# A mixture-of-experts stage whose gathered rows are split into fp16 halves before they are turned instead of after

## The chip, the cores and the metric

The kernel runs on one core of one Trainium2 chip. The metric is the device time of one execution in microseconds. The kernel before takes 682.88 us (median of 3 runs, 682.84 to 685.06).

## The reference

The input is `x`, 16 batches of 224 rows of 512 fp32 numbers. Two blocks follow each other, each with a residual and a gate `tanh(g)`:

```
x = x + tanh(g_xattn) * attention_like(layernorm(x))     # two products with a context of 750 rows per batch, gelu between them
f = layernorm(x)                                         # 3584 rows of 512
scores = softmax(f @ gate_w); top 2 of 8 experts
y = sum over the 2 experts e of a row:  ( silu((s*f) @ w1[e]) * ((s*f) @ w3[e]) ) @ w2[e]      # 512 -> 256 -> 512
x = x + tanh(g_ffn) * y
```

`s` is the score of the row for that expert. The change lies in the second block.

## The kernel before

The kernel has two phases. In the first, a loop over 16 batches does the attention-like block, norms the rows a second time, chooses the experts and writes the normed rows `xf` and a route table to DRAM. In the second phase, 63 blocks of 128 rows, each of one expert, go through the expert's three matrices. Blocks 0 to 26 are written out one by one (`PEEL2 = 27`), and what is left of the last batches (routing, second norm, the map of the later blocks) is put between them (`between(b)`); blocks 27 to 62 run in a loop of 12 blocks per turn.

fp32 accuracy from fp16 matmuls comes from halves: a number is scaled, its fp16 rounding is the one half (index 0, called high in the code's names) and what the rounding left over is the other (index 1, low). Every product is three fp16 matmuls (`PARTS`).

For a block `b` the engines do this, each in its own written order, held together by semaphores:

- SP loads the block's rows of the route table (`load_meta`, a register load of the block's place and a DMA of 1 KB). It runs ahead through a ring of 12 slots and waits for the scatter (`added`) that frees a slot.
- GpSimd (POOL) gathers the 128 rows from DRAM into one of 4 buffers `xg` (L525), 4 blocks ahead, and later adds the finished rows to the output in DRAM (L537, the scatter).
- TensorE turns the fp32 rows in four 128x128 pieces into a PSUM bank (`trans_rows`, L1323), one block ahead, then turns the hidden rows of the block before (`trans_hid`, L1357), does the 12 matmuls up of this block (`up`, L1368) and the 6 down of the block before (`down`, L1377).
- ScalarE copies the turned rows from PSUM into the half 0 (`rows_high`, L735), applies silu to the result of `up` (L777) and copies the result of `down` out with a scale (`y_out`, L766).
- VectorE waits for `y_ready` of two blocks ago, loads the expert's number, makes the scales (L1146, L1147), takes the low half of the hidden rows (`hid_low`, L1137), the low half of the turned rows (`rows_low`, L1074, from PSUM), and then multiplies silu with the other half of `up` (L1155, the hidden rows `hh`).

Because `rows_high` and `rows_low` work on block `b + 1` in step `b`, the rows of a block are ready one block ahead. TensorE's next `trans_hid` waits for L1155.

At the change from phase one to phase two SP first loads the table rows of blocks 0 to 3, stores `xf` of batch 14 (`store_norm`), then loads blocks 4 to 11 (L378 to L382).

Of the kernel before, what the change touches and what calls it, by code (L numbers as in the profile page):

```python
# [55 lines left out]
AHEAD = 4  # L56
PEEL2 = 27
APART = 3
MAPPED = 12 * S * TOPK
# [34 lines left out]
def build(nc, x, ctx, g_xattn, g_ffn, gate_w, w1, w2, w3, out):  # L94
# [4 lines left out]
    with st:  # L99
# [35 lines left out]
        ctx_raw = sb("ctx_raw", [P, NC, D])  # L135
        ctx_part = [[sb(f"ctx_part{u}{h}", [CR, NC, D], F16) for h in range(2)] for u in range(2)]
        ctxT_buf = [sb(f"ctxT{u}", [P, 2 * KD * NC * CS], F16) for u in range(2)]
# [62 lines left out]
        y_sb = [ctx_raw[:, AHEAD + u, :] for u in range(2)]  # L200
        xgT = [[ctxT_buf[u][:, h * KD * P:(h + 1) * KD * P] for h in range(2)] for u in range(2)]
        sg, hh = (words[u][:, 1024:1024 + HID].bitcast(F32) for u in range(2))
# [44 lines left out]
        gathered = [sem(f"gathered{a}") for a in range(AHEAD)]  # L247
        xgT_made, xgT_ready = sem("xgT_made"), sem("xgT_ready")
        xgT_high, hhT_high = sem("xgT_high"), sem("hhT_high")
        up_made, sg_ready, hh_ready = sem("up_made"), sem("sg_ready"), sem("hh_ready")  # L250
# [47 lines left out]
        def _(sp):  # L298
# [72 lines left out]
            def load_meta(b, n, half):  # L371

                if not (isinstance(b, int) and b < RING):
# [4 lines left out]
            for b in range(AHEAD):  # L378
                load_meta(b, b, b // 2)
            store_norm(B - 2)  # L380
            for b in range(AHEAD, RING):
                load_meta(b, b, b // 2)  # L382
            store_rows(B - 1)
            store_norm(B - 1)
            for b in range(RING, PEEL2):
                load_meta(b, b % RING, b // 2)
            sp.wait_ge(x2_stored, 16 * B)
            sp.wait_ge(xf_stored, 16 * B)
            sp.wait_ge(map_ready, 2)
            for v in range(2):  # L390
                sp.wait_ge(routed[v], 16 * 2 * TOPK * B // 2)
            sp.nop().then_inc(phase2, 1)
            for b in range(PEEL2, PEEL2 - PEEL2 % RING + RING):
                load_meta(b, b % RING, b // 2)
            with sp.Fori(PEEL2 // RING + 1, NBM // RING) as it:
                for n in range(RING):
                    load_meta(it * RING + n, n, it * (RING // 2) + n // 2)
            for b in range(NBM - NBM % RING, NBM):
                load_meta(b, b % RING, b // 2)
            for u in range(2):  # L400
# [3 lines left out]
        def _(pool):  # L404
# [176 lines left out]
        def _(act):  # L581
# [149 lines left out]

            def rows_high(b, u):

                act.wait_ge(xgT_made, b + 1)
                a.activation(xgT[u][0], T_ps[u][:, :], ACT.Copy, scale=2.0 ** X_BITS).then_inc(xgT_high, 1)  # L735

            def last_step(i, u, h):
# [13 lines left out]
                xfT_out(i * 4 + 1, 1)  # L751
                rows_high(0, 0)

# [14 lines left out]
            def step2(b, n, lap, half):  # L768
                first_, u = isinstance(b, int) and b == 0, n % 2
                if not first_:  # L770
                    hid_high(b - 1)
                rows_high(b + 1, 1 - u)
                act.wait_ge(cols_ready, b + 1)
# [14 lines left out]
        def _(dve):  # L788
# [281 lines left out]

            def rows_low(b, u):

                dve.wait_ge(xgT_high, b + 1)
                v.scalar_tensor_tensor(xgT[u][1], T_ps[u][:, :], 2.0 ** X_BITS, xgT[u][0], ALU.mult, ALU.subtract).then_inc(xgT_ready, 1)  # L1074

            def last_step(i, u, h):
# [13 lines left out]
                route_scores(i - 3, 1 - u)  # L1090
                rows_low(0, 0)
                route_top(i - 2)
# [46 lines left out]
            def step2(b, n, lap, half):  # L1139
# [23 lines left out]
        def _(pe):  # L1163
# [151 lines left out]

            def trans_rows(b, n, lap):

                u, a = n % 2, n % AHEAD
                pe.wait_ge(gathered[a], lap * (16 * RING // AHEAD) + 16 * (n // AHEAD + 1))
                if not isinstance(b, int) or b >= 2:  # L1320
                    pe.wait_ge(xgT_ready, b - 1)
                for k in range(KD):
                    ins = t_.transpose(T_ps[u][:, k * P:(k + 1) * P], xg[a][:, k * P:(k + 1) * P], ident[:, :])  # L1323
                ins.then_inc(xgT_made, 1)

            def last_step(i, u, h):
# [13 lines left out]
                attend(i, u, 2)  # L1340
                rank(i - 2)

# [16 lines left out]

            def up(b, u, e, first2):  # L1360

                pe.wait_ge(xgT_ready, b + 1)
                if not first2:
                    pe.wait_ge(hh_ready, b - 1)
                for m, (k, part) in enumerate((k, part) for k in range(KD) for part in PARTS):
                    rows = xgT[u][part[0]][:, k * P:(k + 1) * P]
# [30 lines left out]
            def step2(b, n, lap, half):  # L1397
                u = n % 2
                if isinstance(b, int) and b == 0:
                    loaded[0] = expert(0)  # L1400
                    pe.wait_ge(w_split, 3 * E)
                    up(0, 0, loaded[0], True)
                    return
# [3 lines left out]
                loaded[0] = e_up  # L1407
                trans_rows(b + 1, n + 1, lap)
                trans_hid(b - 1)
                up(b, u, e_up, small and b < 2)  # L1410
                down(b - 1, 1 - u, e_down, small and b - 1 < 2)
# [34 lines left out]
```

## Time and profile before

| what | value |
|---|---|
| median of 3 runs | 682.88 us |
| the profiled execution | 682.06 us, of which the span of the trace is 680.4 us |
| TensorE | 632.9 us busy, 93% of the span |
| ScalarE | 459.6 us, 68% |
| VectorE | 416.5 us, 61% |
| GpSimd | 396.6 us, 58% |
| phase two | from about 368.6 us (first matmul up) to the end |

The span is the time that the trace covers; 1.66 us of the profiled execution lie outside it. An engine's busy time says little about its share in the end time; the chain that ended last, in order of time, says which engine each stretch waited for.

### The profile page before, as it was taken

What the parts mean: (1) busy time and instruction counts of PE and PEld (TensorE: products, weight loads), DVE (VectorE), ACT (ScalarE), POOL (GpSimd) and SP (SyncE); (2) the same over time, 40 slices, a digit from 0 to 9 for tenths busy, and PEclk for the clock granted to TensorE, in tenths of its full rate; (3) what the DMA queues carried; (4) which work ended last, traced back from release to release, by engine and by line L of the source; (5) the groups of instructions that cost most, each with busy time, mean ns of one, the idle gap of its engine ahead of it and who ended that gap; (6) DMA issues with size and microseconds to landing.
All of it is one profiled execution on the core that took longest, in us unless ns stands there. A gap on an engine that the chain in (4) does not pass through costs nothing.

```text
span 680.4 us, 15835 instructions
## 1 busy us (share of the span) xinstructions
PE 632.9 (93%) x4638; PEld 443.5 (65%) x4639; DVE 416.5 (61%) x1287; ACT 459.6 (68%) x771; POOL 396.6 (58%) x460
## 2 busy tenths in 40 slices
PE   2789999999999999999998999999999999999990
PEld 1677788788887888878875555555555545555540
DVE  3468788988889888898896644553333333333330
ACT  5899999899999999999974344444434434434440
POOL 4332347765676556665567587776546555665561
PEclk9999999999999999999999999999999999999996
DMA  7455558656776658656424576566666667666663
GB/s 213 134 173 154 157 159 192 185 155 154 193 173 170 185 129 222 168 159 186 127 90 106 106 126 110 105 108 120 121 121 108 118 117 123 108 113 119 110 115 53
DMA packets 51604, 95.04 MB, mean 140 GB/s; under 512 B 17184, under 2 KB 25504, under 8 KB 51536
## 3 DMA queue, kind: packets, MB, share of 16 engines
q1 hardware_dynamic: 34240, 60.02, 33.2%
q0 software_dynamic: 16480, 34.15, 28.1%
q8 instruction: 36, 0.59, 0.4%
q14 instruction: 32, 0.26, 0.2%
q10 hardware_dynamic: 816, 0.02, 0.1%
HBM read 62.15 MB, written 32.01 MB: 138 GB/s over the span
## 4 chain that ended last, share of the span: by engine, by line
PE 39%; DMA 5%; DVE 3%; issue 2%; ACT 1%; POOL 1%; DVEq 0%; SPq 0%; POOLq 0%; ACTq 0%
PE bank L1368 21%; PE bank L1377 11%; DMA out_rows<-ctx_raw,meta 4%; PE bank L1323 4%; PE bank L1357 2%; DMA ctx_raw<-xf_rows,meta 1%; DMA meta<-route_table 0%; PE bank L1257 0%; PE bank L1222 0%; DVE ctx_part L825 0%; POOL out_rows L537 0%; DVEq L1145 0%; ACT ctx_part L624 0%; ACT ctx_raw L766 0%; DVE x L863 0%
## 5 line engine op out<-in xcount | busy, mean ns | idle before, releaser
L1368 PE MATMUL bank<-w,ctxT 128*128 x756 | 173.5, 379 | 0.6 <-issue 0.6
L537 POOL DMA_INDIRECT out_rows<-ctx_raw,meta x63 | 100.3, 1592 | 94.0 <-DMA out_rows<-ctx_raw,meta 77.5
L1222 PE MATMUL bank<-ctx_part,a_part 125*112 125x512 f16 x576 | 135.1, 380 | 0.8 <-DVE a_part L834 0.8
L1368 PEld LDWEIGHTS bank<-w,ctxT 128*128 128x128 f16 x756 | 73.9, 98 | 75.7 <-issue 0.7
L1210 PE MATMUL bank<-xnT,ctxT 128*125 128x224 f16 x1152 | 117.7, 261 | 0.3 <-ACT ctxT L629 0.3
L1210 PEld LDWEIGHTS bank<-xnT,ctxT 128*125 128x125 f16 x1152 | 111.9, 138 | 0.4 <-issue 0.4
L777 ACT ACTIVATE ctxT<-bank,cols 128x256 f32<-128x256 f32 x63 | 29.9, 474 | 115.0 <-issue 90.0
L1222 PEld LDWEIGHTS bank<-ctx_part,a_part 125*112 125x112 f16 x576 | 71.4, 130 | 39.6 <-DVE a_part L834 0.8
L629 ACT ACTIVATE ctxT<-bank 128x1000 f16<-128x1000 f16 x96 | 94.5, 1006 | 2.5 <-PE bank L1177 2.5
L1377 PE MATMUL bank<-w2s,ctxT 128*128 x378 | 91.9, 379 | 1.4 <-DVE ctxT L1137 1.3
L489 POOL DMA_INDIRECT route_table<-route,pos_i x64 | 72.7, 1136 | 18.2 <-issue 18.2
L525 POOL DMA_INDIRECT ctx_raw<-xf_rows,meta x67 | 67.3, 1005 | 21.0 <-issue 17.7
L1146 DVE TENSOR_SCALAR cols<-Q,meta 128x2 f32 x63 | 15.0, 238 | 104.4 <-ACT ctx_raw L766 64.3
L766 ACT ACTIVATE ctx_raw<-bank,cols 128x512 f32<-128x512 f32 x63 | 43.4, 688 | 52.2 <-PE bank L1377 52.2
L1155 DVE SCALAR_TENSOR_TENSOR ctxT<-bank,cols,ctxT 128x256 f32<-128x256 f32 x63 | 30.5, 484 | 62.8 <-issue 49.5
L1377 PEld LDWEIGHTS bank<-w2s,ctxT 128*128 128x128 f16 x378 | 36.9, 98 | 46.5 <-issue 4.8
L825 DVE SCALAR_TENSOR_TENSOR ctx_part<-ctx_raw,ctx_s,ctx_part 125x1024 f16<-125x1024 f32 x48 | 60.3, 1272 | 8.3 <-ACT ctx_part L624 8.3
L834 DVE SCALAR_TENSOR_TENSOR a_part<-a_f,factors,a_part 125x448 f16<-125x448 f32 x48 | 32.8, 683 | 37.1 <-ACT a_part L643 37.0
L1177 PE MATMUL bank<-ident,ctx_part 125*128 125x125 f16 x768 | 53.6, 220 | 1.6 <-ACT ctxT L629 1.1
L624 ACT ACTIVATE ctx_part<-ctx_raw,ctx_s 125x1024 f16<-125x1024 f32 x48 | 53.1, 1135 | 1.9 <-POOL ctx_s L444 1.9
L1177 PEld LDWEIGHTS bank<-ident,ctx_part 125*128 125x128 f16 x768 | 48.1, 99 | 8.2 <-issue 1.3
L594 ACT ACTIVATE ctx_part<-ctx_raw 125x1024 f16<-125x1024 f32 x48 | 50.3, 1048 | 1.1
(155 smaller groups left out, 986.8 us busy)
## 6 DMA issues: line engine op xcount, KB each, us to landing
ctx_raw<-in_ctx SPq DMA_DIRECT2D x48, 448.0 KB
w_raw<-in_L_ffn_w SPq DMA_DIRECT2D x24, 512.0 KB, 6.3
x<-in_x SPq DMA_DIRECT2D x16, 448.0 KB, 6.5
out_rows<-x SPq DMA_DIRECT2D x16, 448.0 KB
xf_rows<-xf SPq DMA_DIRECT2D x16, 448.0 KB, 4.6
ctx_raw<-in_ctx SPq DMA_DIRECT2D x48, 52.0 KB
meta<-route_table SPq DMA_DIRECT2D x67, 1.0 KB, 2.5
ctx_raw<-xf_rows,meta POOLq DMA_INDIRECT x67, 4.2
```

What stands on the lines that cost most here:

```text
L489: g.indirect_dma_start(out=table, out_offset=bass.IndirectOffsetOnAxis(ap=pos_i[v][:, m:m + 1], axis=0), in_=route[v][:, t, k, :], in_offs ...
L525: g.indirect_dma_start(out=xg[n % AHEAD], out_offset=None, in_=src, in_offset=bass.IndirectOffsetOnAxis(ap=meta[n][:, 0:1], axis=0)).then_ ...
L537: g.indirect_dma_start(out=out, out_offset=bass.IndirectOffsetOnAxis(ap=meta[n][:, 0:1], axis=0), in_=y_sb[n % 2], in_offset=None, compute ...
L594: a.activation(ctx_part[i % 2][1][:, 2 * q:2 * q + 2, :], ctx_raw[0:CR, 2 * q:2 * q + 2, :], ACT.Square, accum_out=ctx_sum[0:CR, q:q + 1]) ...
L624: a.activation(ctx_part[u][0][:, c, :], ctx_raw[0:CR, c, :], ACT.Copy, scale=ctx_s[u][0:CR, q:q + 1].bitcast(F32)).then_inc(ctx_high, 1)
L629: a.activation(ctxT[u][:, :, c * CS:c * CS + CR], T_half[c % 2], ACT.Copy).then_inc(ctxT_ready, 1)
L825: v.scalar_tensor_tensor(ctx_part[u][1][:, c, :], ctx_raw[0:CR, c, :], ctx_s[u][0:CR, q:q + 1].bitcast(F32), ctx_part[u][0][:, c, :], ALU. ...
L1177: ins = t_.transpose(T_half[c % 2][:, h * KD + k, :], ctx_part[u][h][:, c, k * P:(k + 1) * P], ident16[0:CR, 0:CR])
L1210: ins = t_.matmul(dst, ctxT[u][:, hc * KD + k, c * CS:c * CS + CR], xnT[u][:, hx, k, :], start=j == 0, stop=j == KD * len(PARTS) - 1)
L1222: ins = t_.matmul(O_ps[t][0:TT, :], a_part[ha][:, c, t * TT:(t + 1) * TT], ctx_part[u][hc][:, c, :], start=c == 0 and (ha, hc) == PARTS[0] ...
L1368: ins = t_.matmul(H_ps[u][:, :], rows, w, start=m == 0, stop=m == KD * len(PARTS) - 1)
L1377: ins = t_.matmul(O_ps[u][:, :], rows, w2s[:, bass.ds(e * (KH * 2 * D) + (2 * k + part[1]) * D, D)], start=m == 0, stop=m == KH * len(PART ...
```

## The change

The order of splitting and turning is exchanged. The gathered fp32 rows are now split first, as rows, in SBUF: ScalarE writes the half 0 into `xh[.][:, 0, :]` (`rows_high`) and VectorE the half 1 into `xh[.][:, 1, :]` (`rows_low`), two blocks ahead (`SPLIT = 2`) in two buffers. The half 0 is turned by four fp16 transposes on TensorE (`turn_high`), into PSUM as fp16, and VectorE copies it out (`high_out`). The half 1 is turned by one transposing DMA per block, from SBUF to SBUF, issued by SP (`turn_rows`). The turned rows `xgT` have three buffers instead of two. SP's loop over the blocks is written out in full; it issues the turning DMA of block `b + 2`, then the table row of block `b + 8` (`META = 8`). The first 12 table rows all come before `store_norm` of batch 14.

```diff
+SPLIT = 2
+META = 8
...
+        xh = [ctx_part_buf[0][0][:, 2 * u:2 * u + 2, :] for u in range(2)]
+        xgT_buf = [ctxT_buf[0][:, r * 2 * KD * P:(r + 1) * 2 * KD * P] for r in range(3)]
...
+        T_rows = [t[:, :].bitcast(F16)[:, 0:KD * P] for t in T_ps]
...
+            def turn_rows(b, n):
+                sp.wait_ge(rows_split, b + 1)
+                if b >= 3:
+                    sp.wait_ge(up_made, b - 2)
+                sp.dma_start_transpose(xgT[n % 3][1].rearrange("p (g r) -> p g r", g=KD), xh[n % 2][:, 1, :]).then_inc(xgT_loaded[n % 3], 16)
...
+            for b in range(RING):
                 load_meta(b, b, b // 2)
             store_norm(B - 2)
+            for b in range(SPLIT):
+                turn_rows(b, b)
+            for b in range(PEEL2):
+                turn_rows(b + SPLIT, b + SPLIT)
...
+                if b + META >= RING:
+                    load_meta(b + META, (b + META) % RING, (b + META) // 2)
+            for b in range(PEEL2, NB):
+                if b + SPLIT < NB:
+                    turn_rows(b + SPLIT, (b + SPLIT) % RING)
+                if b + META < NBM:
+                    load_meta(b + META, (b + META) % RING, (b + META) // 2)
...
             def step2(b, n, lap, half):
-                pool.wait_ge(xgT_made, b + 1)
+                pool.wait_ge(rows_split, b + 1)
...
-                act.wait_ge(xgT_made, b + 1)
-                a.activation(xgT[u][0], T_ps[u][:, :], ACT.Copy, scale=2.0 ** X_BITS).then_inc(xgT_high, 1)
+            def rows_high(b, n, lap):
+                act.wait_ge(gathered[n % AHEAD], lap * (16 * RING // AHEAD) + 16 * (n // AHEAD + 1))
+                if n >= SPLIT:
+                    act.wait_ge(high_turned, b - 1)
+                    act.wait_ge(rows_split, b - 1)
+                a.activation(xh[n % 2][:, 0, :], xg[n % AHEAD], ACT.Copy, scale=2.0 ** X_BITS).then_inc(rows_cast, 1)
...
-                v.scalar_tensor_tensor(xgT[u][1], T_ps[u][:, :], 2.0 ** X_BITS, xgT[u][0], ALU.mult, ALU.subtract).then_inc(xgT_ready, 1)
+            def high_out(b, n):
+                dve.wait_ge(high_turned, b + 1)
+                if n >= 3:
+                    dve.wait_ge(up_made, b - 2)
+                v.tensor_copy(xgT[n % 3][0], T_rows[n % 2]).then_inc(highT_ready, 1)
+            def rows_low(b, n, lap):
+                dve.wait_ge(rows_cast, b + 1)
+                if n >= SPLIT:
+                    dve.wait_ge(xgT_loaded[(n - SPLIT) % 3], lap * (16 * RING // 3) + 16 * ((n - SPLIT) // 3 + 1))
+                v.scalar_tensor_tensor(xh[n % 2][:, 1, :], xg[n % AHEAD], 2.0 ** X_BITS, xh[n % 2][:, 0, :], ALU.mult, ALU.subtract).then_inc(rows_split, 1)
...
-                rows_low(b + 1, 1 - u)
+                rows_low(b + SPLIT, n + SPLIT, lap)
+                high_out(b + 1, n + 1)
...
-                    ins = t_.transpose(T_ps[u][:, k * P:(k + 1) * P], xg[a][:, k * P:(k + 1) * P], ident[:, :])
-                ins.then_inc(xgT_made, 1)
+            def turn_high(b, n):
+                pe.wait_ge(rows_cast, b + 1)
+                if n >= 2:
+                    pe.wait_ge(highT_ready, b - 1)
+                for k in range(KD):
+                    ins = t_.transpose(T_rows[n % 2][:, k * P:(k + 1) * P], xh[n % 2][:, 0, k * P:(k + 1) * P], ident16[:, :])
+                ins.then_inc(high_turned, 1)
...
-                for b in range(2):
-                    trans_rows(b, b, 0)
                 attend(i, u, 2)
+                for b in range(SPLIT):
+                    turn_high(b, b)
...
-                pe.wait_ge(xgT_ready, b + 1)
+                pe.wait_ge(highT_ready, b + 1)
+                pe.wait_ge(xgT_loaded[n % 3], lap * (16 * RING // 3) + 16 * (n // 3 + 1))
```

VectorE, one block of the loop of phase two, before (`bank` is PSUM, `ctxT` holds the turned halves and the hidden rows):

```order
L1147 COPY cols<-Q 128x1
L1137 TENSOR_TENSOR ctxT<-bank,ctxT 128x256
L1073 REGISTER_ALU
L1074 SCALAR_TENSOR_TENSOR ctxT<-bank,ctxT 128x512
L1155 SCALAR_TENSOR_TENSOR ctxT<-bank,cols,ctxT 128x256
```

The same place now (`ctx_raw` holds the gathered rows, `ctx_part` the split rows):

```order
L1179 COPY cols<-Q 128x1
L1169 TENSOR_TENSOR ctxT<-bank,ctxT 128x256
L1101 REGISTER_ALU
L1104 SCALAR_TENSOR_TENSOR ctx_part<-ctx_raw,ctx_part 128x512
L1097 COPY ctxT<-bank 128x512
L1188 SCALAR_TENSOR_TENSOR ctxT<-bank,cols,ctxT 128x256
```

A copy of 128x512 out of PSUM has come between the split of the rows and the product L1155 (now L1188), and the split reads SBUF instead of PSUM.

SP at the change of phases, before, from the table row of block 3 on (each `load_meta` is four such rows):

```order
L375 TENSOR_LOAD bmap
L375 ISA x2
L376 ISA
L376 DMA meta<-route_table 128x2
L339 DMA xf_rows<-xf 112x1024
L375 TENSOR_LOAD bmap
L375 ISA x2
L376 ISA
L376 DMA meta<-route_table 128x2
```

The same engine now, from the table row of block 11 on:

```order
L382 TENSOR_LOAD bmap
L382 ISA x2
L383 ISA
L383 DMA meta<-route_table 128x2
L346 DMA xf_rows<-xf 112x1024
L390 DMA_TRANSPOSE ctxT<-ctx_part 128x4x128 x3
L341 DMA out_rows<-x 112x1024
L390 DMA_TRANSPOSE ctxT<-ctx_part 128x4x128 x4
```

Eight table rows have moved ahead of the store, and the first turning DMA stands behind all twelve of them.

## Rows read from the trace of the kernel before

**Rows 1.** Stretch, length, busy PE, PEld, DVE, ACT, POOL; clock, DMA share, GB/s

```profile
495.00:640.00 145.00, 143.31 (x758) 76.78 (x757) 53.36 (x157) 61.86 (x126) 80.75 (x63) 1.00 0.66 114
```

**Rows 2.** Chain that ended last, one block of the loop: start us, us, what

```profile
564.96 1.29 PE bank L1377 x6
566.25 0.44 PE bank L1323 x4
566.69 0.22 PE bank L1357 x2
566.91 2.59 PE bank L1368 x12
```

**Rows 3.** Timeline, fp16 transposes of phase one: start us, us, engine, line

```profile
342.07 0.61 PE L1177 MATMUL bank<-ident,ctx_part 125*128 125x125 f16 x8
...
347.40 1.04 PE L1177 MATMUL bank<-ident,ctx_part 125*128 125x125 f16 x16
```

**Rows 4.** Timeline, one block of the loop, all engines, [idle before <-releaser]

```profile
559.98 1.58 POOL L537 DMA_INDIRECT out_rows<-ctx_raw,meta  x1 [2.84 <-DMA out_rows<-ctx_raw,meta]
...
564.31 1.58 POOL L537 DMA_INDIRECT out_rows<-ctx_raw,meta  x1 [1.45 <-DMA out_rows<-ctx_raw,meta]
...
565.61 0.48 DVE L1155 SCALAR_TENSOR_TENSOR ctxT<-bank,cols,ctxT 128x256 f32<-128x256 f32 x1 [0.69 <-issue]
...
566.09 0.60 PE L1323 MATMUL bank<-ident,ctx_raw 128*128 128x128 f32 x4
566.20 0.99 POOL L525 DMA_INDIRECT ctx_raw<-xf_rows,meta  x1 [0.30 <-issue]
...
567.22 0.60 ACT L735 ACTIVATE ctxT<-bank 128x512 f16<-128x512 f32 x1
567.99 0.23 DVE L1146 TENSOR_SCALAR cols<-Q,meta 128x2 f32 x1 [1.90 <-ACT ctx_raw L766]
...
568.52 0.68 DVE L1074 SCALAR_TENSOR_TENSOR ctxT<-bank,ctxT 128x512 f16<-128x512 f32 x1
```

**Rows 5.** Groups by line, phase one: operations whose operands lie in SBUF

```profile
L834 DVE SCALAR_TENSOR_TENSOR a_part<-a_f,factors,a_part 125x448 f16<-125x448 f32 x42 | 28.7, 683 | 35.0 <-ACT a_part L643 35.0
L643 ACT ACTIVATE a_part<-a_f,factors 125x448 f16<-125x448 f32 x42 | 28.0, 668 | 1.4
```

**Rows 6.** Timeline, SP's issues at the change of phases

```profile
355.00 3.75 SPq L376 DMA_DIRECT2D meta<-route_table  x4
358.92 0.33 SPq L339 DMA_DIRECT2D xf_rows<-xf  x1
360.03 9.03 SPq L376 DMA_DIRECT2D meta<-route_table  x8
```

**Rows 7.** Chain that ended last, matmuls up of blocks 0 and 1

```profile
368.56 2.77 PE bank L1368 x12
372.98 2.59 PE bank L1368 x12
```

**Rows 8.** DMA issues of the whole run: KB each, median us to landing

```profile
w_raw<-in_L_ffn_w SPq DMA_DIRECT2D x24, 512.0 KB, 6.3
...
gate<-in_L_ffn_gate_w ACTq DMA_DIRECT2D x1, 16.0 KB, 8.7
```

**Rows 9.** DMA queues and issues, 480 to 600 us

```profile
q0 software_dynamic: 5763, 13.52, 63.1%
q1 hardware_dynamic: 3880, 0.03, 2.4%
...
meta<-route_table SPq DMA_DIRECT2D x26, 1.0 KB, 3.5
ctx_raw<-xf_rows,meta POOLq DMA_INDIRECT x26, 4.2
```

**Rows 10.** Timeline, a block with map work on VectorE between two blocks

```profile
441.58 0.60 PE L1323 MATMUL bank<-ident,ctx_raw 128*128 128x128 f32 x4
...
444.16 0.23 DVE L1146 TENSOR_SCALAR cols<-Q,meta 128x2 f32 x1 [0.77 <-DVE xn L1018]
```

More of the change, by code:

```diff
@@ L135, in build @@
         ctx_raw = sb("ctx_raw", [P, NC, D])
-        ctx_part = [[sb(f"ctx_part{u}{h}", [CR, NC, D], F16) for h in range(2)] for u in range(2)]
+        ctx_part_buf = [[sb(f"ctx_part{u}{h}", [P, NC, D], F16) for h in range(2)] for u in range(2)]
+        ctx_part = [[b[0:CR, :, :] for b in of_batch] for of_batch in ctx_part_buf]
         ctxT_buf = [sb(f"ctxT{u}", [P, 2 * KD * NC * CS], F16) for u in range(2)]
@@ L200, in build @@
         y_sb = [ctx_raw[:, AHEAD + u, :] for u in range(2)]
-        xgT = [[ctxT_buf[u][:, h * KD * P:(h + 1) * KD * P] for h in range(2)] for u in range(2)]
-        sg, hh = (words[u][:, 1024:1024 + HID].bitcast(F32) for u in range(2))
+        xh = [ctx_part_buf[0][0][:, 2 * u:2 * u + 2, :] for u in range(2)]
+        xgT_buf = [ctxT_buf[0][:, r * 2 * KD * P:(r + 1) * 2 * KD * P] for r in range(3)]
+        xgT = [[b[:, h * KD * P:(h + 1) * KD * P] for h in range(2)] for b in xgT_buf]
+        sg, hh = (words[1][:, 1024 + n * HID:1024 + (n + 1) * HID].bitcast(F32) for n in range(2))
         hhT = [ctxT_buf[0][:, 4096 + h * KH * P:4096 + (h + 1) * KH * P] for h in range(2)]
@@ L247, in build @@
         gathered = [sem(f"gathered{a}") for a in range(AHEAD)]
-        xgT_made, xgT_ready = sem("xgT_made"), sem("xgT_ready")
-        xgT_high, hhT_high = sem("xgT_high"), sem("hhT_high")
+        rows_cast, rows_split, hhT_high = sem("rows_cast"), sem("rows_split"), sem("hhT_high")
+        high_turned, highT_ready = sem("high_turned"), sem("highT_ready")
+        xgT_loaded = [sem(f"xgT_loaded{r}") for r in range(3)]
         up_made, sg_ready, hh_ready = sem("up_made"), sem("sg_ready"), sem("hh_ready")
@@ L371, in load_meta @@
             def load_meta(b, n, half):
-                if not (isinstance(b, int) and b < RING):
+                if b >= RING:
                     sp.wait_ge(added[n % 2], half * 16 - (RING // 2 - 1) * 16)
@@ L376, in load_meta @@
                 sp.dma_start(meta[n][:, :], table[bass.ds(row * P, P), :]).then_inc(meta_loaded[n], 16)
-            for b in range(AHEAD):
+            def turn_rows(b, n):
[4 more added lines that the diff above has]
+            for b in range(RING):
                 load_meta(b, b, b // 2)
@@ L380, in _ @@
             store_norm(B - 2)
[L381 to L399, printed above, removed]
+            for b in range(SPLIT):
+                turn_rows(b, b)
+            for b in range(PEEL2):
+                turn_rows(b + SPLIT, b + SPLIT)
+                if b == 0:
+                    store_rows(B - 1)
+                elif b == 4:
+                    store_norm(B - 1)
+                if b + META == PEEL2:
+                    sp.wait_ge(x2_stored, 16 * B)
+                    sp.wait_ge(xf_stored, 16 * B)
+                    sp.wait_ge(map_ready, 2)
+                    for v in range(2):
+                        sp.wait_ge(routed[v], 16 * 2 * TOPK * B // 2)
+                    sp.nop().then_inc(phase2, 1)
+                if b + META >= RING:
+                    load_meta(b + META, (b + META) % RING, (b + META) // 2)
@@ L751, in last_step @@
                 xfT_out(i * 4 + 1, 1)
-                rows_high(0, 0)
+                for b in range(SPLIT):
+                    rows_high(b, b, 0)
             last_step(B - 1, 1, (B - 1) // 2)
@@ L771, in step2 @@
                     hid_high(b - 1)
-                rows_high(b + 1, 1 - u)
+                rows_high(b + SPLIT, n + SPLIT, lap)
                 act.wait_ge(cols_ready, b + 1)
@@ L1090, in last_step @@
                 route_scores(i - 3, 1 - u)
-                rows_low(0, 0)
+                for b in range(SPLIT):
+                    rows_low(b, b, 0)
+                high_out(0, 0)
                 route_top(i - 2)
@@ L1337, in last_step @@
                 rows_norm2(i - 1, 1)
-                for b in range(2):
-                    trans_rows(b, b, 0)
                 attend(i, u, 2)
+                for b in range(SPLIT):
+                    turn_high(b, b)
                 rank(i - 2)
@@ L1365, in up @@
                 for m, (k, part) in enumerate((k, part) for k in range(KD) for part in PARTS):
-                    rows = xgT[u][part[0]][:, k * P:(k + 1) * P]
+                    rows = xgT[n % 3][part[0]][:, k * P:(k + 1) * P]
                     w = w13[:, bass.ds(e * (KD * 4 * HID) + (2 * k + part[1]) * 2 * HID, 2 * HID)]
@@ L1401, in step2 @@
                     pe.wait_ge(w_split, 3 * E)
-                    up(0, 0, loaded[0], True)
+                    up(0, 0, 0, 0, loaded[0], True)
                     return
@@ L1407, in step2 @@
                 loaded[0] = e_up
-                trans_rows(b + 1, n + 1, lap)
+                turn_high(b + 1, n + 1)
                 trans_hid(b - 1)
-                up(b, u, e_up, small and b < 2)
+                up(b, n, lap, u, e_up, small and b < 2)
                 down(b - 1, 1 - u, e_down, small and b - 1 < 2)
```

10 lines of the change are left out of this document (1 added, 9 removed).

## The prediction

> **What bounds the kernel now.** I read the busy time by stretch first, then the chain that ended last, then the timeline of one block, then the DMA views. In the stretch of the block loop TensorE is busy for 143.31 of 145.00 us at a granted clock of 1.00, VectorE and ScalarE for well under half, and the 16 DMA engines for a share of 0.66 [rows 1]. The chain of a block in the loop holds nothing but TensorE: 1.29 us of `down`, 0.44 of the four fp32 transposes of the gathered rows, 0.22 of the two of the hidden rows, 2.59 of `up`, in all 4.54 us per block [rows 2]. So phase two lasts as long as TensorE's instructions do, 63 blocks of it, and whatever is taken from them is gained until another loop becomes the longer one.
>
> I measure one block from its first transposition, at 566.09 [rows 4]; the block before began 4.54 earlier, at 561.55.
>
> **TensorE.** Removed are four fp32 transposes per block, 0.44 us or 0.11 each [rows 2]. Added are four fp16 ones of the same size. Phase one has fp16 transposes of 125x128: 8 take 0.61 us and 16 take 1.04, so one more costs (1.04 - 0.61) / 8 = 0.054 us [rows 3], and four cost 0.22. A block becomes 4.54 - 0.22 = 4.32 us. Over the 36 blocks of the loop that is 7.9 us, over 26 of the written-out blocks 5.7.
>
> **VectorE** gains a copy of 128x512 fp16 numbers out of PSUM. The nearest row is L1074, which reads the same PSUM tile in fp32 and one operand more, 0.68 us [rows 4]; that is the upper end, half of it, 0.34, the lower (half the bytes), and I take 0.6, near the row. The split itself now reads SBUF: L834 does that with 448 columns in 0.683 us, so 512 take up to 0.78, and at least the 0.68 of L1074 [rows 4, 5]; I take 0.73. L1074 starts 2.43 us into the block. The product L1155 can then start at 2.43 + 0.73 + 0.6 = 3.76, with both upper ends at 3.89. Before, L1155 started at 565.61 - 561.55 = 4.06 after 0.69 us of idling for silu [rows 4]; with `up` 0.22 earlier it could start at 3.84. It takes 0.48 and ends at 4.32 to 4.37; TensorE wants it at 4.32 + 0.22 = 4.54. So in the loop the copy is hidden under the wait for silu and costs nothing; without that cover it would cost up to its 0.68. In the written-out blocks the cover is thinner. With map work put between two blocks L1146 came 444.16 - 441.58 = 2.58 us into the block instead of 1.90 [rows 4, 10], 0.68 late. Before, that was absorbed by the 0.69 of idling; now L1155 would end at 3.76 + 0.68 + 0.48 = 4.92, or 0.38 after TensorE wants it. Work of VectorE is put between in 13 of these blocks where it is not trivial, some of it short enough to be free: I take 0.25 on the average, 13 x 0.25 = 3.2 us given back (from 0 to 13 x 0.5 = 6.5).
>
> **ScalarE** splits from SBUF instead of PSUM: 0.60 now [rows 4], up to 0.668 x 512 / 448 = 0.76 from L643 [rows 5]; it idles for over half of the stretch [rows 1], so nothing.
>
> **The gather** loses lead, since the rows are split two blocks ahead. It starts 0.11 into a block (566.20) and lands 4.2 us later [rows 4, 9], thus 4.31 into a block that will last 4.32. `rows_high` takes the rows at 567.22, 1.13 into the next block, 0.91 after the shortening: 0.9 us of slack. Where a scatter waits for the one before it (2.84 us instead of 1.45, rows 4) the gather behind it is 1.4 us late, `rows_high` ends at 0.91 + 0.5 + 0.76 = 2.17, still before VectorE wants it at 2.43. That leaves 0.26 for more DMA traffic; for the blocks where this is not enough I put 1.0 us (0 to 4).
>
> **The turning DMA** is what no row shows. Let L be the time from the end of `rows_low` to its landing. SP issues it two blocks ahead of `up`. `rows_low` ends 2.43 + 0.73 = 3.16 into a block, `up` starts 0.44 into the block two later, so L may be 2 x 4.32 + 0.44 - 3.16 = 5.9 us at no cost. If it is more, `up` waits, and three blocks take 3.16 + L + 2.59 + 1.29, so a block takes 2.35 + L / 3; at L = 6.6 the whole gain in the loop is gone. The rows: in this stretch 1 KB lands in 3.5 us and a gather of 256 KB in 4.2, of which 0.99 is GpSimd's own part [rows 4, 9]; over the whole run 512 KB take 6.3 and the slowest load is 8.7 [rows 8]. This DMA moves 128 KB from SBUF to SBUF, between 1 and 256 KB, so I take 4.0 us, with ends at 3.5 and 8.7. SP has the time: a table row costs it 9.03 / 8 = 1.13 us [rows 6], and its place in the order before a turning DMA waits only for a scatter of four blocks before.
>
> A page of the Trainium skill speaks against it: "VectorE: DVE Perf Modes", section "The three transpose paths", gives 1309 ns for a 128x128 tile through the DMA crossbar and advises TensorE where PSUM will do. By an estimate from it four tiles one behind the other take 5.2 us, and with the 3.5 of a small landing L would be 8.7, the far end of the first rival. "Advanced Engine Details and Errata", section "X-Bar Transpose (TRN2)", says that such DMAs are as fast as regular ones; by that L would be my 4.0. No run here shows either yet.
>
> **The DMA engines' share.** They are busy for 0.66 x 4.54 = 3.0 us of each block [rows 1]. The turning DMA adds t. A packet of the gathers and scatters takes 63.1% x 16 x 120 us / 5763 = 0.21 us for 2.3 KB, a table packet of 8 bytes 2.4% x 16 x 120 / 3880 = 0.012 us [rows 9]. By bytes, 128 KB are 56 large packets, t = 56 x 0.21 / 16 = 0.7 us. In 512 pieces of 256 bytes it is 0.4 to 6.7 us, at the one price and the other. I take 0.7, since the bytes are those of the nearest row; 3.7 of 4.32 us then fit.
>
> **The change of phases.** Before, the table rows of 4 blocks left SP from 355.00 to 358.75, then the store, then 8 more in 9.03 us from 360.03 [rows 6]. Now all twelve come first: 358.75 + 0.78 for the first register load + 9.03 = 368.56, the store 0.5, and the first turning DMA leaves at 369.2 although its rows are split some 4 us earlier. At L = 4.0 the first `up` starts at 373.2. Before it started at 368.56 [rows 7]. That is 4.6 us lost (4.1 at L = 3.5, 9.3 at 8.7), and nothing returns it, since TensorE bounds all that follows; blocks 0 and 1 stay 4.42 apart as before, because there TensorE waits for L1155.
>
> **The sum** against the profiled execution (682.06 us: span 680.4 and 1.66 around it): -7.9 - 5.7 + 3.2 + 4.6 + 1.0 = -4.8, 677.3. The median of the runs shown is 682.88, 0.8 above, so I forecast 678.0; own range 673 to 683.
>
> **Rival 1, slower: the turning DMA lands late.** Its place is `up`'s wait for `xgT_loaded`; it decides from L = 6.6 on. At L = 7.5 a block takes 4.85: 62 x 0.31 = 19 us, and 8.1 at the change of phases, which makes 710. At 8.7 it is 5.25: 62 x 0.71 + 9.3, which makes 736. For it: the engines that would carry it are two thirds busy, and 1 KB already needs 3.5 us there. Against: 256 KB need only 0.7 more.
>
> **Rival 2, slower: the DMA engines are full.** From t = 1.3 on the block lasts 3.0 + t. At t = 2 it takes 5.0: 62 x 0.46 + 5 makes 716; at 6.7 over 1000. For it: a transposition may go in small pieces. Against: the small packets here are cheap.
>
> **Rival 3: the gain is eaten.** L = 5.5 loses 6.1 at the change of phases, the between work 6.5, the gathers 1.5: -13.6 + 14.1, which makes 683, no change. For it: three of the five terms are losses of about the gain's size. Against: the loop of 36 blocks has none of that work.
>
> **Chances.** Forecast 0.50, rival 1 0.24, rival 2 0.08, rival 3 0.18. A measurement here can tell about 0.5% from no change, so faster means under 679.5 and slower over 686.3. Of the forecast's half some three quarters lie under 679.5: faster 0.39. The rest of it and most of rival 3: same 0.28. Rivals 1 and 2 and a rest: slower 0.33. The range from 672 to 716 leaves out a few hundredths below, and above it the far ends of rivals 1 and 2, some 0.15.
>
> **What would show it.** In the chain of the changed kernel a block of the loop should read 1.29, 0.22, 0.22, 2.59. The turning DMA's median time to landing should be 3.5 to 5.5 us; over 6 with TensorE waiting for it in `up` is rival 1, a DMA share above 0.95 rival 2. The first `up` should start at about 373. L1188 should wait for silu in the loop, and not in the written-out blocks with work between. I am wrong if the blocks of the loop are longer than 4.4 us or if the first `up` is not late.

## The result and the profile after

The changed kernel takes 699.67 us (median of 4 runs, 692.31 to 703.86) against 682.86 for the kernel before: a ratio of 1.020, 95% interval 1.016 to 1.024. The longest of the four runs is set apart as slow, and the ratio leaves it out. The change makes the kernel slower by 17 us; 678.0 and faster was forecast. The profiled execution is the lowest of the four, 692.31 with a span of 690.6, so the profile shows 10.2 of the 17 us.

Where they lie is read from the starts of the first weight load of `up` (us; the last two columns give the time from the start in block 1 to that in block 27, and from there to that in block 62):

| | first `up` | second `up` | blocks 1 to 27 | blocks 27 to 62 |
|---|---|---|---|---|
| before | 368.5 | 372.7 | 124.8 | 160.5 |
| after | 372.9 | 378.7 | 128.4 | 160.8 |

Up to the second `up` 6.0 us are lost, in the written-out blocks 3.6, in the loop 0.3 where 7.7 should have been gained.

The loop's chain first. Where nothing is late, a block of the changed kernel reads as forecast (chain that ended last: start us, us, what), and this answers to [rows 2]:

```profile
520.30 0.22 PE bank L1355 x4
520.52 0.22 PE bank L1389 x2
520.75 2.59 PE bank L1401 x12
523.34 1.31 PE bank L1410 x6
```

That is 4.34 us, and the quickest blocks start 4.24 apart. But TensorE is no longer busy throughout. The stretches of after (length, busy PE, PEld, DVE, ACT, POOL; clock, DMA share, GB/s); the last answers to [rows 1]:

```profile
372.00:440.00 68.00, 64.17 (x363) 33.92 (x363) 37.78 (x140) 24.99 (x50) 45.24 (x37) 0.97 0.78 125
440.00:495.00 55.00, 49.63 (x262) 24.55 (x261) 26.77 (x90) 23.40 (x47) 36.33 (x30) 0.97 0.88 138
495.00:640.00 145.00, 140.05 (x755) 68.41 (x753) 64.76 (x192) 62.49 (x125) 86.81 (x63) 1.00 0.85 144
```

In the loop TensorE idles for 5 us instead of 1.7, and the DMA engines' share went from 0.66 to 0.85. The queues and issues from 480 to 600 us, as in [rows 9]:

```profile
q0 software_dynamic: 5898, 13.79, 67.5%
q1 hardware_dynamic: 17793, 3.42, 18.9%
...
meta<-route_table SPq DMA_DIRECT2D x27, 1.0 KB, 4.0
```

18.9 - 2.4 = 16.5% of 16 engines for 120 us are 317 us for some 26 turning DMAs, 0.76 us of all 16 engines each: t, 0.7 in the prediction, is as forecast. From 3880 to 17793 packets are 13913 for 26, about 512 each of 256 bytes, at 317 / 13913 = 0.023 us apiece.

Who waits for what tells the rest. In the trace of before, ScalarE's `y_out` waits for no scatter between 440 and 640. Of the waits of that stretch (us in total, times, longest) the first row is of before, the others of after:

```profile
POOL out_rows L537 <- DMA out_rows<-ctx_raw,meta: 62.3, 32, 2.9
...
POOL out_rows L554 <- DMA out_rows<-ctx_raw,meta: 32.5, 13, 4.2
ACT ctx_raw L787 <- DMA out_rows<-ctx_raw,meta: 21.6, 14, 4.0
ACT ctx_part L755 <- DMA ctx_raw<-xf_rows,meta: 9.9, 11, 1.8
```

GpSimd's wait for its own earlier scatters is not new: it was 62.3 us before and is 32.5 after. New are the two rows below it. The first of them is `y_out`, held because the scatter of two blocks ago has not landed yet and its buffer is not free; the other is the cast of the gathered rows (`rows_high`), which waits for the gather. The costliest block, 14, shows how the wait of `y_out` reaches TensorE (timeline: start us, us, engine, what, [idle before <-releaser]):

```profile
434.13 1.62 POOL L554 DMA_INDIRECT out_rows<-ctx_raw,meta  x1 [2.68 <-DMA out_rows<-ctx_raw,meta]
...
437.54 2.75 PE L1401 MATMUL bank<-w,ctxT 128*128 x12
...
440.51 0.69 ACT L787 ACTIVATE ctx_raw<-bank,cols 128x512 f32<-128x512 f32 x1 [3.98 <-DMA out_rows<-ctx_raw,meta]
...
442.60 0.23 DVE L1178 TENSOR_SCALAR cols<-Q,meta 128x2 f32 x1 [2.95 <-issue]
...
442.80 0.42 DVE L1169 TENSOR_TENSOR ctxT<-bank,ctxT 128x256 f16<-128x256 f32 x1
...
443.36 1.70 PE L1410 MATMUL bank<-w2s,ctxT 128*128 x6 [3.06 <-DVE ctxT L1169]
```

Read from the bottom: `down` waits 3.06 us for the hidden rows' second half (L1169). That stands behind `cols` on VectorE, which may not overwrite its tile before `y_out` has read it; 1.4 us pass between the end of `y_out` (441.20) and `cols`, for the register load of the expert's number. `y_out` waits 3.98 us for a scatter that itself left late, at 434.13, after 2.68 us of waiting for the scatter before, and took 6.3 us. So block 14 starts 8.06 us after block 13. Scatters take 4.87 us to land before (median of blocks 27 to 62, from GpSimd's start) and 5.30 after.

The change of phases, TensorE and SyncE; SyncE's first rows answer to [rows 6], `up`'s to [rows 7]:

```profile
366.33 0.61 PE L1355 MATMUL bank<-ident,ctx_part 128*128 128x128 f16 x8
369.02 0.22 PE L1298 MATMUL bank<-M,lower 112*112 112x16 f16 x1 [2.08 <-DVE R L921]
...
372.91 4.36 PE L1401 MATMUL bank<-w,ctxT 128*128 x12 [3.62 <-DMA ctxT<-ctx_part]
...
378.77 2.75 PE L1401 MATMUL bank<-w,ctxT 128*128 x12
```
```profile
355.58 13.02 SPq L383 DMA_DIRECT2D meta<-route_table  x12
368.64 0.43 SPq L346 DMA_DIRECT2D xf_rows<-xf  x1
369.12 5.56 SPq L390 DMA_TRANSPOSE ctxT<-ctx_part  x3
```

The twelve table rows are out at 368.6, the turning DMA leaves at 369.12, lands 3.55 us later in the chain, and `up` starts at 372.91. Then it takes 4.36 us instead of 2.76. The stretches around it show why: a clock of 0.50, the lower level of 1.2 GHz, from 369.4 to 376.2. It fell just after a wait of 2.08 us that before did not have: TensorE's `rank` (L1298) waits for VectorE's `route_top`, which now stands behind two splits and a copy instead of one split. The clock falls a second time for 3.4 us from 444.45, 1.1 us after the wait of 3.06 us at block 14 has ended; that is the 0.97 of the stretch from 440 to 495, and block 15 starts 5.51 us after block 14.

```profile
355.00:369.00 14.00, 11.94 (x83) 8.70 (x82) 11.13 (x44) 8.90 (x16) 8.41 (x9) 1.00 0.33 78
369.40:376.20 6.80, 3.29 (x8) 1.26 (x9) 1.56 (x6) 0.00 (x0) 5.69 (x5) 0.50 0.66 164
376.30:383.00 6.70, 5.70 (x35) 2.93 (x34) 4.05 (x13) 1.99 (x5) 0.00 (x0) 1.00 0.55 127
```

### The profile page after: what moved, and what is told of

It is laid out like the page before. It is cut to its first block, busy times and chain, and to the rows that moved or that the text cites. A ratio compares the mean times of both kernels' runs of the same rounds, so it can differ in the third digit from the quotient of the medians.

```text
span 690.6 us, 16173 instructions
## 1 busy us (share of the span) xinstructions
PE 628.1 (91%) x4638; PEld 428.6 (62%) x4639; DVE 438.2 (63%) x1352; ACT 461.2 (67%) x772; POOL 404.7 (59%) x460
## 4 chain that ended last, share of the span: by engine, by line
DMA 17%; PE 11%; issue 8%; POOL 7%; DVE 4%; POOLq 2%; ACT 2%; SPq 2%; DVEq 1%; ACTq 0%
DMA out_rows<-ctx_raw,meta 14%; PE bank L1401 6%; POOL out_rows L554 4%; PE bank L1410 3%; POOLq L550 2%; POOL ctx_raw L542 2%; DMA x<-in_x 1%; DMA ctx_raw<-xf_rows,meta 1%; ACT ctx_raw L787 1%; SPq L382 1%; SPq L383 1%; DVE ctx_part L846 1%; PE bank L1389 1%; DVEq L1177 1%; DMA ctxT<-ctx_part 1%
## 5 line engine op out<-in xcount | busy, mean ns | idle before, releaser
L1401 PE MATMUL bank<-w,ctxT 128*128 x756 | 176.2, 383 | 4.2 <-DMA ctxT<-ctx_part 3.6
L554 POOL DMA_INDIRECT out_rows<-ctx_raw,meta x63 | 107.0, 1698 | 94.3 <-DMA out_rows<-ctx_raw,meta 49.5
L755 ACT ACTIVATE ctx_part<-ctx_raw 128x512 f16<-128x512 f32 x65 | 40.7, 628 | 15.0 <-DMA ctx_raw<-xf_rows,meta 13.8
```

The lines of the kernel that those rows point to most:

```text
L554: g.indirect_dma_start(out=out, out_offset=bass.IndirectOffsetOnAxis(ap=meta[n][:, 0:1], axis=0), in_=y_sb[n % 2], in_offset=None, compute ...
```

## The experiments

Each ratio is to runs of the kernel before in the same job. The other columns are read from the profiled execution as above. The four executions of the changed kernel lie up to 11.6 us apart, those of `lead6`, `turn_first`, `y4` and `start_te` 6 to 12 us, so a difference of 3 to 5 us between two of these medians is not clear of noise.

| run | median | ratio, 95% | first, second `up` | 1 to 27 | 27 to 62 |
|---|---|---|---|---|---|
| both_on_te | 690.1 | 1.007 to 1.012 | 371.2, 377.9 | 125.6 | 162.0 |
| before_idle_turn | 688.7 | 1.006 to 1.010 | 369.7, 373.9 | 127.5 | 163.5 |
| lead6 | 696.2 | 1.015 to 1.020 | 375.0, 380.5 | 128.6 | 162.9 |
| turn_first | 696.7 | 1.015 to 1.022 | 369.9, 376.6 | 131.6 | 164.6 |
| y4 | 690.5 | 1.009 to 1.019 | 373.2, 378.9 | 126.5 | 156.5 |
| before_y4 | 682.0 | 0.998 to 1.000 | 368.3, 372.5 | 124.3 | 160.4 |
| start_te | 694.8 | 1.013 to 1.023 | 370.2, 374.3 | 128.9 | 166.2 |
| y4_start | 684.1 | 1.001 to 1.005 | 368.9, 373.1 | 126.1 | 159.4 |
| three | 685.5 | 1.000 to 1.004 | 370.6, 374.8 | 130.4 | 155.7 |
| three_swap | 685.7 | 1.001 to 1.006 | 369.2, 373.4 | 133.2 | 156.5 |
| three_m8 | 684.2 | 0.997 to 1.002 | 368.9, 373.1 | 127.4 | 156.5 |
| before_idle_y4 | 686.3 | 1.002 to 1.006 | 369.6, 373.8 | 126.2 | 162.3 |
| cut27 | 683.0 | 1.000 to 1.004 | 368.7, 372.8 | 124.8 | 161.0 |
| cut27_y4 | 679.1 | 0.993 to 0.997 | 367.8, 372.0 | 124.8 | 159.3 |
| cut27_three | 678.4 | 0.993 to 0.996 | 368.3, 372.4 | 124.4 | 157.0 |

**both_on_te**: the changed kernel without the turning DMA; both halves turned by eight fp16 transposes.

```
-  sp.dma_start_transpose(xgT[n % 3][1]..., xh[n % 2][:, 1, :])
+  for h in range(2):  t_.transpose(T_rows[n % 2][:, (h*KD + k)*P:...], xh[n % 2][:, h, k*P:...], ident16)
-  v.tensor_copy(xgT[n % 3][0], T_rows[n % 2])
+  v.tensor_copy(xgT_buf[n % 3], T_rows[n % 2])
```

> The changed kernel without its turning DMA: both fp16 halves of a block are turned on TensorE (8 transposes, 0.44 us, so a block's TensorE work is 4.54 us as before), VectorE copies both out; the split two blocks ahead stays. Theory traffic (the turning DMA's packets delay scatters and gathers): scatters land in 4.9 us again, blocks of the loop last 4.54 to 4.6, total 680 to 686. Theory lead (splitting two blocks ahead leaves the gathers too little lead, and ScalarE waits for them in order): gathers are still awaited at landing, blocks of the loop last 4.7 or more, total over 690.

690.1, above the traffic theory's range and at the edge of the other's. Its DMA share is 0.65, and still the loop takes 1.5 us and the start 5.2 more than before. So some 7 of the 17 us come without the DMA: from the split ahead of the transposes, and at the start, where `up` comes at 371.2 and runs at half speed. The scatters don't land in 4.9 us again either, as the traffic theory had it: the median of blocks 27 to 62 is 5.17, and `y_out` waits for them for 6.7 us between 440 and 640 (21.6 in the changed kernel). So part of the scatters' lateness comes without the turning DMA; what causes it in this run stays open.

**before_idle_turn**: the kernel before, and per block one turning DMA that nobody reads (SyncE's order follows the change).

```
+  sp.dma_start_transpose(idle[b % 3]..., w13[:, 0:D])
```

> The kernel before with one turning DMA of 128x512 fp16 numbers per block added on SP that nobody reads. Theory traffic: scatters land in 5.3 us or more and the kernel is 5 to 15 us slower than before. Theory lead: scatters may land later, but the gathers still have some 9.5 us from issue to use, so the time stays within 2 us of before.

688.7, +5.5 on its own runs of before, at the low end of the traffic's 5 to 15. By the table its profiled execution loses 1.2 us ahead of the first `up`, mostly in phase one, 2.7 in the written-out blocks and 3.0 in the loop. The DMA share and issues of this run:

```profile
495.00:640.00 145.00, 142.26 (x745) 74.91 (x744) 52.71 (x156) 60.93 (x124) 79.91 (x62) 1.00 0.84 140
```
```profile
ctxT<-w SPq DMA_TRANSPOSE x26, 4.4
out_rows<-ctx_raw,meta POOLq DMA_INDIRECT x26, 5.7
meta<-route_table SPq DMA_DIRECT2D x25, 1.0 KB, 4.0
```

The traffic makes the others late with nothing else changed but SyncE's order, and `y_out` waits for scatters between 440 and 640, where before it waits for none:

```profile
ACT ctx_raw L780 <- DMA out_rows<-ctx_raw,meta: 17.2, 12, 2.3
```

**lead6**: the changed kernel with gathers six ahead.

```
-AHEAD = 4
+AHEAD = 6
```

> The changed kernel with six gather buffers instead of four (two of them in memory that phase one no longer needs), so each gather is issued two blocks earlier. Theory lead: ScalarE no longer waits for gathers, blocks of the loop last 4.3 to 4.4, 8 to 14 us less than the changed kernel. Theory traffic: the scatters still land late and hold the output buffers, gain under 3 us.

696.2, 3 less than the changed kernel, with overlapping intervals. Between 440 and 640 the cast no longer waits for a gather, and `y_out` waits for scatters as in the changed kernel. The theory that the gathers' lead was the cause, which asked for 8 to 14 us, falls.

```profile
ACT ctx_raw L789 <- DMA out_rows<-ctx_raw,meta: 23.6, 14, 4.1
```

**turn_first**: the first turning DMA ahead of the last four table rows.

```
-  for b in range(RING):   load_meta(b, b, b // 2)
+  for b in range(AHEAD):  load_meta(b, b, b // 2)      # then the store, then four more, then turn_rows(0)
```

> The changed kernel with 8 instead of 12 table rows ahead of the first turning DMA; the other four come in the block loop. If SP's order causes the late start, the first turning DMA leaves at about 366 instead of 369 us, the first matmul up starts at about 370 instead of 372.9, TensorE's clock does not fall there, and the total is 4 to 5 us below the changed kernel. If something else sets the start (the rank of batch 13), under 1.5 us.

696.7, 3 less by the medians, again with overlapping intervals. The first `up` comes 3.0 earlier and the second 2.1, since the clock is halved there again (0.50 for 6.8 us from 368.9), which was not expected. In its profile the blocks are longer by more than that, so the gain doesn't last there: its execution takes 697.8. The wait behind `route_top` is still there, and the one for the turning DMA is down to 0.96 us; `both_on_te`, which has no turning DMA, has the first wait too (third row), and its clock fell at 370.3:

```profile
368.64 0.22 PE L1299 MATMUL bank<-M,lower 112*112 112x16 f16 x1 [2.08 <-DVE R L922]
...
369.87 5.30 PE L1402 MATMUL bank<-w,ctxT 128*128 x12 [0.96 <-DMA ctxT<-ctx_part]
...
369.30 0.22 PE L1295 MATMUL bank<-M,lower 112*112 112x16 f16 x1 [2.13 <-DVE R L918]
```

So the clock falls without the long wait for the turning DMA.

**y4**: the changed kernel with four output buffers; the wait for the scatter of two blocks ago moves to GpSimd.

```
-  act.wait_ge(added[u], half * 16)          # y_out, from block 2
+  act.wait_ge(added[u], half * 16 - 16)     # from block 4
+  hold(pool, added[n % 2], half * 16)       # scatter
```

> The changed kernel with four output buffers in place of two; the wait for the scatter of two blocks ago moves from ScalarE's y_out to GpSimd's scatter. Theory 'output buffers' (a scatter that lands late holds y_out, behind it VectorE's cols and the hidden rows, and so TensorE's down): blocks 1 to 62 get back most of what they lost, the loop falls from 160.8 us toward 36 x 4.35 = 157, the 26 written-out blocks from 128.4 toward 123; 687 to 693 in all. Rival 'rate of the scatters' (each scatter now takes 5.3 us, and at changes of expert the next has to wait for it, so that GpSimd's own queue falls behind whatever the buffers): 696 to 702, no shorter blocks, and the wait seen at y_out moves to the scatter.

690.5, 9 less than the changed kernel by the medians and 5.4 less by the profiled executions (686.94 against 692.31); the intervals of the two ratios just overlap. The loop falls to 156.5, under the 160.5 of before. The waits show a new one coming up, the cast for its gather, 25.4 us where it was 9.9:

```profile
ACT ctx_part L757 <- DMA ctx_raw<-xf_rows,meta: 25.4, 23, 3.4
POOL out_rows L556 <- DMA out_rows<-ctx_raw,meta: 24.3, 10, 3.2
...
ACT ctx_raw L790 <- DMA out_rows<-w_raw,meta: 4.6, 5, 1.3
```

So late scatters did hold the output buffers. Two further pairs of runs below, in which this edit is the only difference, are clear of noise: `start_te` against `y4_start`, 694.8 to 684.1, and `cut27` against `cut27_y4`, 683.0 to 679.1.

**before_y4**: the same edit on the kernel before.

> The kernel before with the same four output buffers. If its y_out waits for scatters too, 1 to 4 us less than before (679 to 682); if, as its trace suggests (y_out 2 to 4 us after the scatter of two blocks ago has landed, in the first blocks), it has slack there, 682 to 684.

682.0, no change: there two buffers are enough.

**start_te**: the first two blocks turned as before.

```
-  sp: turn_rows(0), turn_rows(1)
+  t_.transpose(T_ps[b][:, k*P:...], xg[b][:, k*P:...], ident)      # b = 0, 1, split from PSUM
```

> The changed kernel, but the first two blocks are turned as before (f32 rows on TensorE, split from PSUM); the turning DMAs begin with block 2. Theory 'change of phases' (the first turning DMA on the path, and the halved clock after TensorE's wait of 3.6 us): first up back at 368.5 and second at 372.7, no half speed near 370; 693 to 695 in all, 5 to 6 less than the changed kernel. Rival (as where the turning DMA was only moved ahead of the table rows: the gain at the start is given back in the next blocks, since these are set by the scatters): 697 to 701.

694.8, the expected number and 5 less than the changed kernel, but the intervals overlap, and in its profile the 4.4 us gained at the second `up` are lost again behind it (a loop of 166.2). The halved clock at the start is gone, and so are the waits of 2.08 and 3.62 us; no run takes away the first of them alone. The first `up` is still 1.6 later than before. In this kernel it also waits for a signal of SyncE's queue that I put behind the table rows; in `y4_start`, which starts in the same way, that leaves it 0.4 later, and the rest here is a phase one that ended 1.2 later than there:

```profile
370.16 2.76 PE L1412 MATMUL bank<-w,ctxT 128*128 x12 [1.19 <-SPq L396]
```

**y4_start**: both edits.

> Both edits together, four output buffers and the first two blocks turned as before. If both theories hold: 680 to 687, a loop of 157 to 159 and a first up at 368.5. If the scatters' rate sets the blocks: 693 to 700.

684.1. The two gains add up within the noise (9 and 5, together 15.6), and here each is clear of it: the start gives 6.4 us on top of `y4`, the buffers 10.7 on top of `start_te`. They were two causes. The kernel is still not faster than before.

**three**: and gathers six ahead, table rows nine ahead.

```
-AHEAD = 4
-META = 8
+AHEAD = 6
+META = 9
```

> Four output buffers and the first two blocks turned as before, and now gathers six blocks ahead in place of four (the table rows nine ahead). In the run with the first two edits ScalarE's cast still waited 24.6 us for gathers between 440 and 640 (21 times), and silu and y_out stand behind it. Theory 'the lead of the gather is the next limit, once the output buffers are not': these waits go, the 35 blocks from 27 to 62 fall from 159.4 to 153 to 156, and the time to 676 to 681, under the kernel before. Rival 'nothing is left but the scatters' order at changes of expert': 682 to 686, as with two edits, since six ahead alone had given 3 us and left 23.6 us of y_out's waits.

685.5. The loop falls as hoped, to 155.7, but blocks 14 to 22 lose more; block 21 starts 7.82 us after block 20. SyncE's queue there has 8.6 us between two turning DMAs (its timeline; the last row is the wait that ended in between, at 470.6):

```profile
463.38 1.30 SPq L390 DMA_TRANSPOSE ctxT<-ctx_part  x1
471.56 0.35 SPq L383 DMA_DIRECT2D meta<-route_table  x1
472.01 2.27 SPq L390 DMA_TRANSPOSE ctxT<-ctx_part  x1
...
SPq L408 <- DMA route_table<-route,pos_i: 5.9, 1, 5.9
```

L408 is the wait, once in the kernel, until all rows of the route table have landed; it stands ahead of the table row of block 27. With table rows nine ahead SyncE comes to it one block earlier, before the route table is ready. The expectation of `three_m8` puts the gap down to a table row that waits for a scatter, and that is not what the trace shows.

**three_swap**: GpSimd's scatter ahead of its gather from block 3 on.

```
+  scatter(b - 1, ...)
   gather(b + AHEAD, ...)
-  scatter(b - 1, ...)
```

> The same, with GpSimd's order turned round from block 3 on: the scatter of the last block first, then the gather six ahead, so that a scatter doesn't stand behind a gather's wait for the split rows (13.5 us in seven waits between 440 and 640 with two edits). If that order held scatters: 1 to 3 us less than with three edits. If the scatters wait for each other instead, the gathers now stand behind that wait and come later: 0 to 3 us more.

685.7, the same: this order isn't what holds the scatters.

**three_m8**: `three` with table rows eight ahead.

> The kernel with three edits (four output buffers, first two blocks turned as before, gathers six ahead), with the table rows eight ahead again. In the run with nine, SyncE's table row of block b+9 waited for the scatter of block b-3, and the turning DMA of the next block stood behind it: 8.6 us between two turning DMAs at 463.4 and 472.0, blocks 20 to 22 of 6.5, 7.8 and 5.9 us. Theory 'SyncE's queue held the turning DMAs': blocks 14 to 22 lose their 10 us, the loop keeps its 155.7; 674 to 679, under the kernel before by 4 to 9. Rival 'the lead of six brings these stalls': 683 to 687 again.

684.2, the rival's number. Blocks 19 to 22 are short now, but 14 to 16 take 7.05, 7.43 and 5.80. Block 15 waits for its own turning DMA, which left at 437.03 and landed 8.84 us later (worked out from the semaphore's events: fifteen of its 16 signals had come after 6.2 us, the last was 2.7 us behind them), in a stretch with a DMA share of 0.92 (chain, and the stretch):

```profile
443.69 2.37 issue
446.07 4.32 PE bank L1415 x12
```
```profile
440.00:495.00 55.00, 52.30 (x279) 25.78 (x278) 27.89 (x85) 22.08 (x45) 36.79 (x29) 0.97 0.92 147
```

The theory of SyncE's queue was right that the queue held the blocks it named, wrong on what held the queue (L408), and wrong on the time: other blocks are late instead.

**before_idle_y4**: the unread turning DMA with four output buffers.

> The kernel before with one unread turning DMA per block (688.7 with two output buffers) and four output buffers (682.0 without the DMA). Theory 'traffic costs time only by scatters that land later than two buffers bear': 682 to 684, the 5 us of the unread DMA gone. Rival 'the traffic delays gathers, table rows and the instruction fetch too': 686 to 689.

686.3, between both numbers: buffers give back 2.4 to 3 of the DMA's 5.5 us. The rest isn't two buffers against four. One part is in its trace: between 440 and 640 TensorE's weight loads for the turning of the rows wait 2.9 us for gathers, where before has no such wait. That is the rival's theory; what else there is stays open.

**cut27, cut27_y4, cut27_three**: the change in the loop alone; blocks 0 to 26 as before.

```
+CUT = 27
+  if b + 1 < CUT:  first_turn(b + 1); first_high(b + 1); first_low(b + 1)      # as before
+  else:            turn_high(b + 1); rows_high, rows_low, high_out, turn_rows
```

> Blocks 0 to 26 turned as before (f32 on TensorE), the split rows and the turning DMA only in the 36 blocks of the loop; two output buffers, gathers four ahead. Theory 'the change pays only where the DMA engines have room and no routing work stands beside the blocks': up to block 27 as before (661 us of span less the loop unchanged), the loop between 157 and 161, as two output buffers still hold y_out there; 680 to 684. Rival 'the turning DMA harms in the loop as elsewhere': a loop of 162 or more, 685 to 690.

> The same with four output buffers. By the first theory the loop falls to 156 to 158 (156.5 with this edit on the changed kernel) and the time to 677 to 681, under the kernel before; by the rival 683 or more.

> The same with four output buffers and gathers six ahead. A loop of 155 to 157 as in the run with nine table rows ahead, 676 to 680 in all if the lead counts in the loop; as with four output buffers alone if it doesn't.

683.0, 679.1 and 678.4. With two buffers the loop gains nothing (161.0 against 160.5), with four 1.2 us, and with gathers six ahead as well 3.5. The last two are faster than both kernels, and their intervals overlap, so that gathers six ahead gain anything in the time is not shown. The best is 0.57% under before (ratio 0.9943, 0.9925 to 0.9960). In its written-out blocks the DMA share stays where it was before (0.68; 0.67 before), in the loop it is 0.84, and the turning DMA lands in 2.9 us:

```profile
440.00:495.00 55.00, 54.86 (x291) 29.42 (x291) 25.34 (x77) 24.56 (x50) 34.88 (x28) 1.00 0.68 119
495.00:640.00 145.00, 141.83 (x774) 70.19 (x772) 65.50 (x193) 63.24 (x129) 89.60 (x65) 1.00 0.84 146
```
```profile
ctxT<-ctx_part SPq DMA_TRANSPOSE x25, 2.9
```

## Why the prediction was wrong

- **TensorE's instructions: right.** The block's chain is 4.34 at the most regular, 4.32 was forecast. As a bound it holds; that TensorE stays the bound did not. The prediction's own sign of being wrong came: the blocks of the loop take 4.59 us on the average (160.8 / 35), more than the 4.4 that it named.
- **The turning DMA's own time: right** in size. L: the median from SyncE's issue to landing is about 4.0 us (2.4 to 6.9, worked out from the semaphores' events), 4.0 was taken; only some six blocks of the changed kernel start right at its landing, block 0 among them, so rival 1 is not the cause, though in `three_m8` at a share of 0.92 a landing of 8.84 shows that its far end exists. Of the two sections named there, the Trainium skill's "Advanced Engine Details and Errata", section "X-Bar Transpose (TRN2)", by which such DMAs are as fast as regular ones, is the closer: 4.0 here, and 4.0 for a table row of 1 KB. The estimate of 8.7 from the Trainium skill's "VectorE: DVE Perf Modes", section "The three transpose paths", is not borne out as a rule.
- **The DMA engines' share: the step that failed.** t was 0.76 against 0.7, and the share 0.85 as "3.7 of 4.32 us then fit" has it (0.86). But it was concluded that what fits costs nothing. Other transfers land later at that share: table rows 4.0 instead of 3.5, scatters 5.30 instead of 4.87. `before_idle_turn` prices this at 5.5 us with nothing else of the change but SyncE's order. For the scatters the share is not the whole cause: in `both_on_te` they take 5.17 at a share of 0.65.
- **The missing term: the scatter.** The prediction priced lateness only for the gather (+1.0). [rows 4] already showed scatters waiting for scatters, 2.84 and 1.45 us; two output buffers had slack enough for 4.87 us and 4.54 per block, not for 5.30 and 4.32, and in `before_idle_turn` not for the later scatters alone, with blocks still at 4.54. `y4` prices it at 9 us by the medians and 5.4 by the profiled executions.
- **The gather's lead: small, as forecast:** 1.0 us was put (0 to 4), `lead6` gives 3, not clear of noise.
- **The change of phases: start right, end wrong.** `up` came at 372.9, 373.2 was forecast. "Blocks 0 and 1 stay 4.42 apart" failed: 6.0 in the chain (372.91 to 378.94), since the clock stood at half for 6.8 us. So the start costs 6.0 instead of 4.6. That `route_top` had moved behind the splits on VectorE, and `rank` with it, was not looked at. `start_te` prices the whole at 5, not clear of noise, `y4_start` against `y4` at 6.4.
- **VectorE's between work:** 3.2 was forecast for the written-out blocks. They lost 3.6 where -2.5 (3.2 - 5.7) was forecast, but at blocks like 14, where the trace shows scatters and not this work. It was not priced by itself. The copy takes 0.42 us, 0.6 was taken, and the split 0.68, 0.73 was taken; VectorE still idles ahead of L1188 (10.9 us in 18 waits between 440 and 640), so in those blocks the copy is hidden, as forecast.

Open is why the median lies 7 us over the profiled execution of the changed kernel, why scatters are late in `both_on_te`, and what holds `cut27_three`'s loop at 157.0: 35 x 0.22 = 7.7 less than before would be 152.8. 1.8 us of it are at the two blocks behind the loop's branch, 39 and 51 (6.22 and 6.18 against 5.47 and 5.15), where TensorE's wait reads only "issue".

## What to carry to other kernels

A transfer that fitted into the DMA engines' free share was not free here: take every other transfer's landing time, lengthen it by what the share allows, and ask of each buffer behind it how much slack it has in the shortened block. When a bottleneck is shortened or transfers are added, the depth of the buffers around it is part of the change. Put such a change where there is room (here the loop, with four buffers), and keep it off the first block after a change of phases, where a single DMA is a chain.

## What the runs showed of the hardware

- In the changed kernel TensorE's granted clock read 0.50 (1.2 GHz) for 6.8 us from 369.4, 0.3 us after a wait of 2.08 us had ended, and at the start of one of 3.62; in `turn_first` from 368.9, after one of 2.08 (ended 368.64); in `lead6` from 370.9, after one of 2.03 (ended 370.19); in `both_on_te` from 370.3, after one of 2.13 (ended 369.30). In `y4_start`, with no wait longer than 1.21 us there, it stayed at 2.4 GHz. A first `up` of 12 matmuls cost 4.38 us instead of 2.77 in the chain.
- A turning DMA of 128x512 fp16 numbers is 512 packets of 256 bytes, 0.76 us of 16 engines, with a median to landing of 2.9 us in `cut27_three` and one landing of 8.84 in `three_m8`, at a share of 0.92; SyncE spends 1.2 us on its issue (median of the changed kernel; 1.30 and 2.27 in the rows of `three`).
